# First expert part of 13 row tiles instead of 15, ranks counted by matrix products, and a denser second routing

## The reference

```python
def _linear_diffusion(h, src, dst):          # six steps, each a mean over the neighbours
    for i in range(1, 7):
        term = (segment_sum(term[src], dst) * inv_deg) / float(i)
        out = out + term
x = x + (_linear_diffusion(silu(layernorm(x) @ W_in.T + b_in)) @ W_out.T + b_out)
# expert layer, E = 8 experts, top 2
xn = layernorm(x) * gamma + beta
logits = xn @ Wr + br
top_vals, top_idx = top_k(logits, 2);  w = softmax(top_vals)
y_e = gelu(xn @ W1[e] + b1[e]) @ W2[e] + b2[e]          # H = 512
x = x + sum over e of y_e * w[e]
```

## Time and profile before

| | us |
|---|---|
| median of three runs | 1309.59 |
| the three runs | 1305.15, 1309.59, 1309.78 |
| time of the profiled execution | 1307.75 |
| its span | 1305.6 |
| PE busy (matmuls) | 1182.4, 91% |
| PE busy (weight loads, beside the matmuls) | 824.2, 63% |
| DVE busy | 726.9, 56% |
| ACT busy | 401.8, 31% |
| POOL busy | 201.5, 15% |

### The profile page before, as it was taken

One profiled execution on the slowest core, in us unless ns is written; L12 is line 12 of the kernel. 1 busy time (PEld: TensorE's weight loads), 2 busy tenths in 40 slices (PEclk: granted clock), 3 DMA queues, 4 the chain that ended last, 5 costly groups with the idle time before them and its releaser, 6 DMA issues.

```text
span 1305.6 us, 27942 instructions
## 1 busy us (share of the span) xinstructions
PE 1182.4 (91%) x7835; PEld 824.2 (63%) x7835; DVE 726.9 (56%) x1533; ACT 401.8 (31%) x785; POOL 201.5 (15%) x245
## 2 busy tenths in 40 slices
PE   5798999999999999999999999978998578898990
PEld 3586776665666666666666666645665367777770
DVE  7889999973444344432543444325556757644555
ACT  2675656550000000000221111101211154464553
POOL 2000000000111111111000000000111154455530
PEclk8998999999999999999999999998999789999995
DMA  6110011014443344323441233112333121122257
GB/s 158 45 50 25 25 37 31 28 37 121 100 99 83 61 109 103 88 55 77 130 129 40 85 108 104 57 29 60 114 112 111 52 86 58 62 71 72 75 151 208
DMA packets 76319, 106.02 MB, mean 81 GB/s; under 512 B 12929, under 2 KB 61880, under 8 KB 76108
## 3 DMA queue, kind: packets, MB, share of 16 engines
q1 hardware_dynamic: 62500, 72.44, 18.8%
q0 software_dynamic: 11376, 25.55, 8.7%
q10 hardware_dynamic: 2356, 6.93, 2.2%
HBM read 76.99 MB, written 37.49 MB: 88 GB/s over the span
## 4 chain that ended last, share of the span: by engine, by line
PE 70%; DVE 12%; issue 9%; DMA 3%; DVEq 2%; ACT 2%; POOL 1%; ACTq 1%; another core or an unknown queue 0%; SPq 0%; POOLq 0%
PE ps L1921 41%; PE ps L1899 7%; PE ps L2084 6%; PE ps L2070 6%; PE ps L1867 4%; DVE v_b L1165 3%; PE ps L1972 2%; POOL v_a L769 1%; PE ps L1835 1%; DMA h_ring<-h_dram 1%; PE ps L2056 1%; DMA adj<-y_dram 1%; PE ps L1846 1%; DVE adj L1072 1%; PE ps L2005 0%
## 5 line engine op out<-in xcount | busy, mean ns | idle before, releaser
L1921 PE MATMUL ps<-v_a,adj 125*125 125x512 f16 x1375 | 297.3, 379 | 0.0
L1921 PE MATMUL ps<-v_b,adj 125*125 125x512 f16 x1250 | 270.2, 379 | 1.8 <-DVE v_b L1190 1.8
L1921 PEld LDWEIGHTS ps<-v_a,adj 125*125 (+1 forms) x1375 | 187.6, 136 | 109.0
L1921 PEld LDWEIGHTS ps<-v_b,adj 125*125 x1250 | 170.6, 136 | 101.2 <-issue 2.2
L894 ACT ACTIVATE t_hi<-ps,cinv 125x256 f32<-125x256 f32 x125 | 59.2, 473 | 454.5 <-PE ps L1921 394.9
L1172 DVE SCALAR_TENSOR_TENSOR t_hi<-ps,cinv,t_hi 125x256 f32<-125x256 f32 x125 | 60.2, 482 | 234.5 <-ACT t_hi L894 234.5
L1165 DVE TENSOR_TENSOR v_b<-v_b 125x2560 f16<-125x2560 f16 x125 | 180.2, 1486 | 6.4 <-PE ps L1867 5.8
L1972 PE MATMUL ps<-v_b,adj 125*125 125x512 f16 x625 | 144.9, 392 | 7.7 <-POOL v_a L746 3.7
L869 ACT ACTIVATE adj<-ps 125x625 f32 (+1 forms) x125 | 112.2, 906 | 66.0 <-PE ps L1867 65.1
L2084 PE MATMUL ps<-adj,v_b 128*128 x672 | 112.8, 275 | 12.7 <-issue 6.1
L1972 PEld LDWEIGHTS ps<-v_b,adj 125*125 125x125 f16 (+1 forms) x625 | 86.4, 141 | 58.6 <-issue 5.5
(11 more groups left out here) (285 smaller groups left out, 977.8 us busy)
## 6 DMA issues: line engine op xcount, KB each, us to landing
h_ring<-h_dram SPq DMA_DIRECT2D x125, 125.0 KB
v_a<-L_ffn_W SPq DMA_DIRECT2D x32, 256.0 KB, 3.4
v_b<-L_ffn_W SPq DMA_DIRECT2D x32, 256.0 KB, 3.6
adj<-w_dram SPq DMA_DIRECT2D x16, 512.0 KB, 5.1
w_dram<-w_hi SPq DMA_DIRECT2D x32, 128.0 KB, 1.9
hx_dram<-h_dram POOLq DMA_DIRECT2D x25, 125.0 KB, 2.5
hx_dram<-x POOLq DMA_DIRECT2D x25, 125.0 KB, 3.3
hx_dram<-L_gnn_b_out POOLq DMA_DIRECT2D x25, 125.0 KB, 4.2
```

The costliest lines, as they stand in the source:

```text
L1921: last = te.matmul(ps[0:NP, u, :], of_tile(adj[0:NP, 0:ADJ], i, u, a * NP, NP), source[:, a, :], start=(a == 0), stop=(a == T - 1))
```

## The change

- TA goes from 15 to 13, FA by it from 22 to 18, FB from 34 to 38. Part A works with CA = 13 columns at a time (two planes), part B with CB = 10 as before.
- `counts` and `prefix` are gone. The one-hot sum `both` becomes fp16, and PE's `ranks` makes the running sums as matrix products: a triangular matrix of halves twice, and for each shift d a matrix of ones times the choices shifted by d tiles, all summed in PSUM; 27 matmuls for part A, 51 for part B (two and four small ones before). DVE copies the ranks.
- `ends_of` is one scan instruction instead of six operations.
- DVE: both choices of part A in slot 20, `place_a` in 21 (waiting for `rt_const` there), `slots`, planes and `experts_of` in 22; `rows_of` stays in 24. POOL makes the constants of part A in slot 21. ACT's `by_partition` of part A stays in slot 23.
- PE: `ranks(0, TA)` ahead of tile 22, part A's `positions` ahead of tile 24, and a wait for `idx_ok` 1 behind the last tile.
- Part B: `place_b` in DVE's `between(9)` (from 10), `slots` and planes in 10 to 12 (from 11 to 14), `experts_of` in 13 (from 15), `rows_of` in 15 (from 16). PE: ranks in 9 (counts in 10 before), positions in 13 and 14 (from 15 to 17).

```diff
-    TA = 15
+    TA = 13
+    CA = 13
@@ POOL, last step
+                if isinstance(i, int) and m == T - 4:
+                    pool.wait_ge(S["tile_ps"], LAST + T - 3)
+                    g.iota(iota_xa, [[1, 128], [0, CA]], base=0, channel_multiplier=0, allow_small_or_imprecise_dtypes=True)
+                    g.memset(ones_8, 1.0)
+                    g.iota(chunk16_a.rearrange("p n c -> p (n c)"), [[T, TOP], [1, TA]], base=0, channel_multiplier=0,
+                           allow_small_or_imprecise_dtypes=True).then_inc(S["rt_const"], 1)
@@ DVE
+                v.tensor_tensor_scan(tiles_b, ones_8, count, 0.0, ALU.mult, ALU.add)
@@ place_a
+                dve.wait_ge(S["rt_const"], 1)
+                v.tensor_copy(rank[:, 0:TA, :], ps[0:NP, 7, 0:TA * NE].rearrange("p (t e) -> p t e", e=NE))
@@ DVE, last step
                 if isinstance(i, int) and m == T - 1:
                     dve.wait_ge(S["tok_ps"], 1)
-                    rows_of(ps[:, 2, 0:PA], 0, FA)
-                    experts_of(FA, ends_a[:, 1:NE + 1], 0)
+                    rows_of(ps[:, POS_BANK, POS_AT:POS_AT + PA], 0, FA)
...
+                if isinstance(i, int) and m == TA + 7:
+                    first_choice(0, TA)
+                    second_choice(0, TA)
+                if isinstance(i, int) and m == TA + 8:
+                    place_a()
+                if isinstance(i, int) and m == TA + 9:
+                    slots(s_top_a, TA)
                     for c in range(GA):
-                        one_plane(planes_a, c, 0, FA, oh_pos_a[c], chunk16_a)
+                        one_plane(planes_a, c, 0, FA, oh_pos_a[c], iota_xa, tile16_a, pin16_a, chunk16_a)
+                    experts_of(FA, ends_a[:, 1:NE + 1], 0)
@@ PE
+            def ranks(t0, t1):
+                at = ps[0:NP, 7, 0:(t1 - t0) * NE]
+                te.matmul(at, half_tri, both[:, t0:t1, :].rearrange("p t e -> p (t e)"), start=True, stop=False)
+                for d in range(1, t1):
+                    t = max(d, t0)
+                    te.matmul(at[:, (t - t0) * NE:(t1 - t0) * NE], ones2[0:NP, 0:NP], both[:, t - d:t1 - d, :].rearrange("p t e -> p (t e)"),
+                              start=False, stop=False)
+                te.matmul(at, half_tri, both[:, t0:t1, :].rearrange("p t e -> p (t e)"), start=False, stop=True)
+                for t in range(t1):
+                    last = te.matmul(ps[:, 7, 256:256 + NE], ones2[0:NP, :], both[:, t, :], start=(t == 0), stop=(t == t1 - 1))
+                last.then_inc(S["cnt_ok"], 1)
...
+                if isinstance(i, int) and m == TA + 9:
                     pe.wait_ge(S["cnt_in"], 1)
+                    ranks(0, TA)
+                if isinstance(i, int) and m == TA + 11:
+                    positions(POS_BANK, POS_AT, planes_a, oh_pos_a, (0, GA), True, True, 0).then_inc(S["tok_ps"], 1)
                 if has(0):
@@ DVE, between
                 if j == 8:
                     second_choice(TA, T)
-                    counts(1, TA, T)
-                if j == 9:
                     v.tensor_tensor(m2, m2, m1, ALU.subtract)
                     v.drain().then_inc(S["ex_in"], 1)
-                    prefix(TA, T)
-                if j == 10:
+                if j == 9:
                     ends_b.append(place_b())
                     places_b()
...
                 if j == 15:
-                    experts_of(FB, ends_b[0], FA)
-                if j == 16:
                     dve.wait_ge(S["tok_ps"], 2)
                     rows_of(ps[:, 6, 0:PB], FA, FB)
@@ PE, between
-                if j == 10:
+                if j == 9:
                     pe.wait_ge(S["cnt_in"], 2)
+                    ranks(TA, T)
+                if j == 13:
+                    positions(6, 0, planes_b, oh_pos_b, (0, 3), True, False, GA)
+                if j == 14:
+                    positions(6, 0, planes_b, oh_pos_b, (3, 5), False, True, GA).then_inc(S["tok_ps"], 1)
```

More of the change, by code:

```diff
@@ L1959, in _, with positions @@
             pe.wait_ge(S["psum_read"], LAST + 5)
+            def positions(bank, col, planes, hots, groups, first, ends, done):
+                for n in range(*groups):
+                    pe.wait_ge(S["rt_done"], done + n + 1)
+                    for c in range(hots[n].shape[2]):
+                        last = te.matmul(ps[:, bank, col:col + planes.shape[2]], hots[n][:, :, c], planes[:, n, :, c],
+                                         start=(first and n == groups[0] and c == 0), stop=(ends and n == groups[1] - 1 and c == hots[n].shape[2] - 1))
+                return last
+            def ranks(t0, t1):
[9 more added lines that the diff above has]
+                last.then_inc(S["cnt_ok"], 1)
             def body(i, u, has):
@@ L1999, in _ @@
             last_step(pe, body)
-            def positions(bank, col, planes, hots, groups, first, ends, done):
-                for n in range(*groups):
-                    pe.wait_ge(S["rt_done"], done + n + 1)
-                    for c in range(CB):
-                        last = te.matmul(ps[:, bank, col:col + planes.shape[2]], hots[n][:, :, c], planes[:, n, :, c],
-                                         start=(first and n == groups[0] and c == 0), stop=(ends and n == groups[1] - 1 and c == CB - 1))
-                return last
-            pe.wait_ge(S["psum_read"], LAST + T + 3)
-            positions(2, 0, planes_a, oh_pos_a, (0, GA), True, True, 0).then_inc(S["tok_ps"], 1)
             def tail_rows(w):
```

140 lines of the change are left out of this document (48 added, 92 removed).

## The result

| | before | after |
|---|---|---|
| median, us | 1308.57 (1305.15 to 1309.78) | 1325.28 (1323.32 to 1325.87) |
| the profiled run's own time, us | 1307.75 | 1323.32 |
| its span, us | 1305.6 | 1321.5 |

The changed kernel is slower: its time is 1.0132 of the kernel before, with a 95% interval of 1.0117 to 1.0148. That is above the range on record, 1302 to 1321, and slower where I had put "same" first.

A forecast was written before the change was run, and what follows sets the result against it. PE, busy 91%, was taken to bound the expert loop, and DVE the seam before it. The terms -2.0 +6.3 -4.9 +8.4 +1.8 -2.0 -4.2 gave +3.4 us, 1313 in the median's terms, range 1302 to 1321.

The forecast's parts named there:

- same: Whole kernel: a time within about 0.5% of no change, 1303 to 1316; chance 0.56.
- starved stretch: Stages 20 and 21: PE idle on issue during POOL's gathers; the burst would fall into PE's stand, -4.2 us.
- DVE stand: Expert loop, PE's 3.95 us wait for DVE's result: place_b starts earlier, the wait goes, with slow clock behind it, -4.9 us.
- seam: Between the sixth diffusion step and the expert loop: first part's routing moved earlier gains 2.0 us.
- fast stages: Expert loop after PE's stand: several stages at 2.96 us rather than 3.4, PE's queue being full, -2.0 us.
- ranks: Behind stage 9 on PE: 51 rank matmuls, 3.8 us, plus a wait for cnt_in of some 2.5, together +6.3 us.
- rival (a): Expert loop: the slow stretch of instructions comes again in another stage, 4.2 us more, 1317; chance 0.25.
- The stand at stage 16: PE ahead of transposed(18): waits for splits, rows_of and the gather of tile 18, +8.4 us (7 to 10).
- The lower clock after it: Expert loop behind PE's stand for the gather: PE runs at a lower clock, +1.8 us (1 to 3).
- Rival (b): Stages 9 to 13: DVE becomes the bound and PE waits for a result, 4 to 6 us more, 1318; chance 0.10.

The follow-up runs named there:

- e9: Kernel before with one gather and one scatter in turn on POOL from the second wait on: 1290.4 us, ratio 1.0001; the kernel before took 1290.39 there.
- e12: e11 with the POOL order of e9: 1290.49 us, ratio 0.9994 to the kernel before.
- e2: Kernel after with POOL's order lighter: three scatters ahead of the second wait, then three gathers, then one of each a stage: 1319.62 us, ratio 1.0089.
- e17: Kernel after, unchanged, beside a kernel before at 1290.73 us: 1303.31 us, ratio 1.0101.
- e1: Kernel after with the second part's rows_of one stage earlier, in DVE's between(14) instead of between(15): 1320.54 us, ratio 1.0086.
- e13: Kernel before, unchanged, run again on one chip with e14: 1308.91 us, ratio 0.999.
- e14: Kernel after, unchanged, run again on one chip with e13: 1326.46 us, ratio 1.013.
- e5: Kernel after with tile 24's matmuls ahead of the first positions on PE: 1325.79 us, ratio 1.0126.
- e8: Kernel after with the edits of e1, e2 and e5 together: 1313.09 us, ratio 1.0038.
- e4: Kernel after's ranks, scan and closer second routing, but the first part with 15 row tiles, placed as in the kernel before: 1310.76 us, ratio 1.0015.
- e16: e11 unchanged, run again beside a kernel before at 1309.16 us: 1310.3 us, ratio 1.0011.
- e10: Kernel after with the second part's rank matmuls one stage later on PE: 1304.27 us, ratio 1.0095.
- e6: Kernel before with the light POOL order of e2: 1310.45 us, ratio 1.0018.
- e7: e4 with the light POOL order of e2: 1314.29 us, ratio 1.0051.
- e11: e4 with the second part's rank matmuls one stage later on PE: 1288.77 us, ratio 0.9983.

## Why the prediction was wrong

The sum was +3.4 and the ledger has +16.1. The 12.7 us between them are: the starved stretch 3.9, S13 to S17 2.4, S0 to S9 1.9, the DVE stand 1.5, the seam 1.4, S21 to S53 1.4, the fast stages 0.8, and the ranks -0.6.

**The starved stretch (-4.2): the step that failed.** I argued that the burst of DMAs would fall into PE's stand, "with its instructions loaded". Half of the picture was right: the burst began in the stand at 1130.85. But it went on until 1144.66, past the stand's end at 1133.70, since four scatters and their gathers had queued up behind the late rows. I had written them down ("scatters 10 to 12 queued behind the gathers") and costed them at nothing. The starved stage came again as stage 17. From S17 to S21 the shortage costs 21.27 - 13.85 = 7.4 us before and 19.78 - 12.68 = 7.1 after, so the term is -0.3. It was also mis-read: stage 20 alone took the 10.8 us that I gave to stages 20 and 21, so what I hoped to win was larger than 4.2. And what stood beside it was a run of seven indirect DMAs, five of them gathers (1129.34 to 1137.24 on POOL), not six gathers in a row. A starved stage that comes again is rival (a), which I gave 0.25. It alone would have made 1317, inside the range; it took the other misses too to reach 1325. The cause of the shortage itself stays open, and no run shows that it is the loading of instructions: no packet of the two instruction queues falls between 1128.5 and 1141.9 in the kernel before, around its starved stage. The Trainium skill ("Runtime: NRT & Kernel Launch", Instruction fetch mechanics) says that a block crossing is mostly hidden. The traces of e9 to e12 hold nothing against that (0.4 to 1.8 us of idle time on issue in the loop); those with the shortage would, at 7 us in one stage, if it were a crossing, which is not shown.

**The stand at stage 16 (+8.4).** Right in place, cause and size: 8.41 for 8.4; 8.39 in e2, 8.42 in e17, and 0.87 when `rows_of` is moved (e1).

**The lower clock after it (+1.8).** Stage 16 takes 5.12 us where a stage after a stand takes 2.9 to 3.3: right. S13 to S17 holds 0.2 us more than my two terms without the shortage, and 2.4 more with it. The positions are 0.7 of that: fifty at 0.149 us where I assumed no change. Another 1.35 lies in S14 to S15 (7.19 for 5.84 in e17), where the granted clock was 0.64 from 1115 to 1119 with PE busy throughout; in e17 it was 1.00 there. Nothing idles on issue in those stages, so whether that dip has to do with the shortage is open.

**Ranks and wait (+6.3).** Measured +5.7, and +5.3 without the shortage: the wait 3.12, the 51 matmuls 2.5 where I took 3.8. They cost 0.05 us each, below my nearest row (0.074) and at the lower bound of the term. The stationary is contiguous and the moving side 8 to 96 columns. The 81 ns of the Trainium skill's pair ("TensorE: Matmul & The Clock Gate", Back-to-back issue gap) was too high here, and its 25 ns too low.

**The DVE stand (-4.9).** Measured -3.4. The stand did not go: 1.51 us were left, ahead of 1106.93. On DVE a plane's three operations, 1104.76 to 1106.29, stand directly ahead of the result that PE waits for there, and ahead of S13 (1107.26); in the kernel before the first plane runs from 1107.66, behind S13 (1103.71). Rival (b) was thus true by that much and not more.

**The seam (-2.0).** Measured -0.6. From the total of tile 20 to S0 the kernel before takes 53.25 us (53.28 in e13), the kernel after 52.82, 52.09 (e14) and 53.36 (e17), so the gain is between nothing and 1.2. The order was as laid out: 1.43 us for `rt_const` (1.7 foreseen), PE idle before the positions (9.35; ten foreseen), tile 24 done behind them. Two durations were off. Tile 24 took 7.80 for 7.3. And slot 22 had a small operation of 1.73 us beside POOL's table; the copies on ACT ended 1.3 us later than laid out. e5 and e8 show what is late next: with the tile first the seam gains 3.1 us more, then the gathers set it.

**Fast stages (-2.0).** Measured -1.2 in e9 and e17, where nothing hides it. My reason, a full queue, no run tried.

**What no term had.** S0 to S9 is +1.9 with the shortage and 0.0 without it; S21 to S53 +1.4 and -0.1. Over the loop the traces with the shortage are longer by 207.09 - 189.84 = 17.3 us in the kernel before and 223.73 - 200.83 = 22.9 in the kernel after. Of the loss of 16.6 us, 5.6 are found only with the shortage and 11.0 without it too. Of those 5.6 the starved stage holds nothing (7.4 and 7.1); they are spread over S0 to S9, the clock at stage 14 and the later stages, and their cause in each place was not tried. S0 to S9 takes 34.48 us in e4 and 32.97 in e16, whose code on PE differs only behind it, so even its place is not understood. My sum without the seam and the starved term was 9.6 for those 11.0, in part by luck: the ranks were priced 1.0 too high, the DVE stand 1.5 and the fast stages 0.8 too well.

So the stand, the largest loss, was priced right, the two gains beside it (seam, DVE stand) too well, and the starved stretch wrong. There I had booked a gain from a cause that I had not established, and gave its failure only 0.25.

## What to carry to other kernels

Price a gain from a stall only where the trace shows what makes the stall; if it is merely seen beside something, let the sum stand without it and keep the gain for the range. When a second part starts earlier, take the index table's last step, here a `rows_of` behind the splits of one tile, and count back from its first reader; moving that one call gave back 0.46 of the 1.32%, some 6 us. A wait taken away gives nothing back where another engine's chain sets the time behind it. In e10 and again in e16 PE no longer waits for the choices and waits for DVE's result instead. When gathers are late, put no scatter ahead of them that itself waits (e6, e7, e8). And where a variant comes out a little faster, look in which stretch: e11's gain looked like its edit's and lay in a seam that the edit doesn't touch.

## What the runs showed of the hardware

The same program takes 1309 us on three chips and 1290.5 on two, each used once. The difference is in the expert loop, 17.3 us from S0 to S53, where PE idles 13.3 us on issue in short gaps of up to 1.2 us on the one kind and 1.8 us on the other (e9). The rest is no such idle time; part of it is the granted clock, 0.84 from S17 to S21 in the one and 1.00 in the other. Ahead of the loop the traces differ by a few us from one execution to the next: S0 of the kernel after came at 1051.55, 1052.11 and 1054.50. A stage of the loop takes 3.60 us in the mean (115.29 by 32) and 3.35 (107.04 by 32).

Fifty-one small matmuls with a contiguous stationary and 8 to 96 columns take 0.05 us each, fifty with a strided one and 76 columns 0.149. A DVE operation on 26 columns took 1.73 us while POOL filled a table, and that table 4.17 instead of 2.71; the two ended together, at 1022.36 and 1022.33, and did the same in e17 (1.73 and 4.16). That each holds up the other is what this looks like; no run tried it. And the granted clock stood at 0.50 for a stretch of 5 us in which PE was busy throughout (e10, 1110 to 1115). The last long wait ahead of it was 2.38 us on DVE at 1099; whether that has to do with it is open.
